# Attention of a decoder layer: 32 tiles one by one against 16 pairs of tiles, with query and scores in PSUM

## The chip, the cores and the metric

The kernel runs on one core of a Trainium2 chip. The metric is the time of one launch in device microseconds. A core has TensorE (matmul; PE in the profile, its weight loads PEld), VectorE (DVE), ScalarE (ACT), GpSimd (POOL) and SyncE (SP), which here issues DMAs.

## The reference

A decoder layer on x of 64 x 64 tokens with 256 features. Three blocks are added to x one after the other: windowed attention, cross-attention over a context, and a mixture of experts. The change touches the first block alone:

```python
Q = (_rmsnorm(x, g) @ _quant_w(wq).T).reshape(Bq, Lq, H, Dh)   # x is layer-normed first; H = Dh = 16
K = (x @ _quant_w(wk).T).reshape(Bq, Lq, H, Dh)
V = (x @ _quant_w(wv).T).reshape(Bq, Lq, H, Dh)
raw = jnp.arange(Lq)[:, None] - jnp.arange(W)[None, :] * STRIDE    # W = STRIDE = 8
valid = raw >= 0
attn = jnp.einsum('blhd,blwhd->bhlw', Q, Kg) * scale               # Kg = K[:, max(raw, 0)]
attn = attn + bias                                                 # -0.5 * log(8 w + 1)
attn = jax.nn.softmax(jnp.where(valid[None, None], attn, -jnp.inf), axis=-1)
out = jnp.einsum('bhlw,blwhd->blhd', attn, Vg).reshape(Bq, Lq, D)
return x + out @ _quant_w(wo).T
```

Every token sees itself and the tokens 8, 16, ... 56 positions before it: a dot product of 16 numbers for each of 16 heads and each lag, a softmax over at most 8 lags, and a weighted sum of values. `_quant_w` turns a weight matrix into -1, 0 and 1 times a scale.

## The kernel before

**Tiles.** 4096 tokens are 4 groups of 8 tiles of 128 tokens. In a group, tile p holds the tokens that stand p strides of 8 into their sequences, so that tile p attends to the tiles 0 to p of its own group. The width w = p + 1 runs from 1 to 8 in every group: 144 widths over the 32 tiles.

**Stages.** A tile goes through nine stages: STAT (mean and variance on VectorE), NORM, TRANS (transpose on TensorE, split into a high and a low part on ScalarE and GpSimd), QKV (ten matmuls into `ps_qk` and `ps_v`, copied out by ScalarE into `qk` and `v_sb`), PROD (`prod` = key times query for w tiles; GpSimd takes about 55% of the w tiles, VectorE the rest, both on line L237; then VectorE sums each run of 16 to `sraw`, L435), SOFT (score times its scale plus bias, L369; maximum over the lags, L379; subtraction, L392; exponential on ScalarE, L291; sum, reciprocal and normalisation, L412, L420, L428), PV (`pv` = value times weight for w tiles on GpSimd, L261), OT (2 w accumulating transposes on TensorE, L460, which add up the w tiles of `pv`), PROJ (output matrix, then VectorE adds the residual `u`, L424).

**Order.** Each engine runs a software pipeline written by hand: step a of group g works on tile n of the first stage, tile n - 1 of the second, and so on. An engine takes its instructions strictly in their written order, and waits at the first whose data isn't there. Counters (`Flow`, `f_...`) tell one engine that another is done. Group 0 and the last eight steps are written out, the groups between run in a loop. SyncE loads x tile by tile, issues the loads of the next phase (`prefetch`) in between, and stores x1 tile by tile.

**Scalars of a tile.** The normalisation needs a power of -0.5 (GpSimd, L275, a 128x2 instruction for each tile) and five 128x1 instructions on VectorE for each tile.

**After attention** an all-engine barrier stands, and then cross-attention and experts, which the change leaves as they are.

Of the kernel before, what the change touches and what calls it, by code (L numbers as in the profile page):

```python
# [21 lines left out]
P = 128  # L22
# [6 lines left out]
SHARE = 0.55  # L29
# [49 lines left out]
def attention_phase(nc, t, prefetch, prefetch_rows):  # L79

    ctx = ExitStack()
    with ctx:
# [3 lines left out]
        def pb(name, shape):  # L86
            return ctx.enter_context(nc.psum_tensor(name, shape, F32))

# [15 lines left out]
        XB = WIN  # L104
        w_raw = sb("w_raw", [P, 4, DC, D])
        w_neg = sb("w_neg", [P, DC, D])

        wq_f = sb("wq_f", [P, DC, D])
# [15 lines left out]
        mv = sb("mv", [P, WIN, 2])
        rs = sb("rs", [P, WIN, 4])
        rq = sb("rq", [P, WIN, 1])
        xh = sb("xh", [P, 2, D])
        u = sb("u", [P, WIN, D])
        qk = sb("qk", [P, 2, WIN, 2, D])
        v_sb = sb("v_sb", [P, 2, WIN, D])  # L130
        prod = sb("prod", [P, 2, WIN, D])
        sraw = sb("sraw", [P, 2, WIN, H])
        nm, rs1 = sb("nm", [P, WIN, 1]), sb("rs1", [P, WIN, 1])
        xt_hi, xt_lo = sb("xt_hi", [P, 2, DC, P], R32), sb("xt_lo", [P, 2, DC, P], R32)
        xt_f, ot = sb("xt_f", [P, 2, DC, P]), sb("ot", [P, 2, DC, P])
# [12 lines left out]

        s_const = sem("s_const")
        s_settled = sem("s_settled")  # L150
        s_wraw = sem("s_wraw")
        s_init = sem("s_init")
        s_wsum = sem("s_wsum")
        s_wtot = sem("s_wtot")
        s_wq = sem("s_wq")
        s_pool0 = sem("s_pool0")
        s_x = [sem(f"s_x{k}") for k in range(XB)]
        f_st = [flow(f"f_st{k}", 16) for k in range(WIN)]
        f_stat, f_rstd, f_xh = flow("f_stat", 4), flow("f_rstd"), flow("f_xh")
        f_rq = flow("f_rq", 2)  # L160
        f_u, f_tr, f_hi, f_lo = flow("f_u"), flow("f_tr"), flow("f_hi", 2), flow("f_lo")
        f_pqk, f_qk, f_v, f_nm = flow("f_pqk"), flow("f_qk"), flow("f_v"), flow("f_nm", 2)
        f_prod_g = flow("f_prod_g")
        f_prod, f_sm, f_exp = flow("f_prod", 2), flow("f_sm", 3), flow("f_exp")
        f_pn, f_pv, f_o = flow("f_pn", 3), flow("f_pv"), flow("f_o")
        f_ot, f_p, f_x1 = flow("f_ot"), flow("f_p"), flow("f_x1")

        def settle(eng):

            eng.sem_inc(s_settled, 1)  # L170

        N_CONST = 3
        w_ready = 12


        STAT, NORM, TRANS, QKV, PROD, SOFT, PV, OT, PROJ = range(9)
        DEPTH = PROJ

        def run(eng, step):

            for a in range(WIN):
                step(0, a, lambda k, a=a: a >= k)
            with eng.Fori(1, GRP) as g:
                for a in range(WIN):
                    step(g, a, lambda k: True)
            for a in range(DEPTH):
                step(GRP, a, lambda k, a=a: a < k)

        def at(g, a, k):

            return 8 * g + (a - k), (a - k) % WIN, g + (a - k) // WIN
# [3 lines left out]
        @block.sync  # L195
        def _(eng):
            open_flows(eng, flows)
            for i, name in enumerate(("wq", "wk", "wv", "wo")):
                eng.dma_start(w_raw[:, i, :, :], t[name].rearrange("(c p) o -> p c o", p=P)).then_inc(s_wraw, 16)
            eng.dma_start(g_col[:, :], t["g"]).then_inc(s_wraw, 16)  # L200
            eng.dma_start(ident[:, :], t["ident"]).then_inc(s_const, 16)
            eng.dma_start(bias_t[:, :, :], t["bias"]).then_inc(s_const, 16)
            eng.dma_start(ones[:, :], t["ones"]).then_inc(s_const, 16)

            def load(g, a):
                f_u.wait(eng, 8 * (g - 1) + a)
                eng.dma_start(x_in[:, a, :], t["x"][g, :, a, :]).then_inc(s_x[a], 16)

            def store(g, a):
                f_x1.wait(eng, 8 * g + a)  # L210
                eng.dma_start(t["x1"][g, :, a, :], u[:, a, :]).then_inc(f_st[a].sem, 16)

            for g in range(2):
                for a in range(WIN):
                    load(g, a)
                if g == 0:
                    prefetch(eng)
            with eng.Fori(2, GRP) as g:
                for a in range(WIN):
                    store(g - 2, a)  # L220
                    load(g, a)
            for a in range(WIN):
                f_st[a].wait(eng, GRP - 3)
            prefetch_rows(eng)
            with eng.Fori(GRP - 2, GRP) as g:
                for a in range(WIN):
                    store(g, a)
            for a in range(WIN):
                f_st[a].wait(eng, GRP - 1)

        def pool_share(v):

            return max(1, round(v * SHARE)) if v > 1 else 0

        def products(e, q, gg, lo, hi):

            return e.tensor_tensor(prod[:, q % 2, lo:hi, :], qk[:, gg % 2, lo:hi, 1, :],  # L237
                                   qk[:, gg % 2, q, 0, :].unsqueeze(1).to_broadcast([P, hi - lo, D]), ALU.mult)

        @block.gpsimd  # L240
        def _(eng):
            e = nc.gpsimd
            e.memset(power[:, :], -0.5).then_inc(s_pool0, 1)
            eng.wait_ge(s_pool0, 1)

            def step(g, a, valid):
                if valid(PROD):
                    m, q, gg = at(g, a, PROD)
                    if pool_share(q + 1):
                        f_qk.wait(eng, m)  # L250
                        f_prod.wait(eng, m - 2)
                        settle(eng)
                        f_prod_g.sig(products(e, q, gg, 0, pool_share(q + 1)))
                if valid(PV):
                    n, p, gg = at(g, a, PV)
                    w = p + 1
                    f_pn.wait(eng, n)
# [1341 lines left out]
```

## Time and profile before

| | us |
|---|---|
| median of 3 runs | 846.86 (846.11 to 847.08) |
| the profiled execution, its own time | 847.12 |
| its span, first to last instruction | 845.3 |
| last addition of the attention phase ends | 239.15 |
| first instruction of the next phase on ScalarE | 242.40 |

In the attention phase the profile's picture in 40 slices shows VectorE at nine tenths or more from the third slice to the tenth, TensorE at five to seven, GpSimd at five to eight. Busy time counts an instruction from its start to its end. A slice's digit is a mean over about 21 us.

### The profile page before, as it was taken

The page shows a single profiled execution, that of the slowest core. Times are in us where ns is not written, and L with a number is a line of the kernel's source. Part 1 is how long each engine was busy: PE and PEld are TensorE (multiplying, and loading weights), DVE is VectorE, ACT ScalarE, POOL GpSimd, SP SyncE. Part 2 cuts the span into 40 slices and gives each one's busy share as a digit, 9 for nine tenths or more (in the row PEclk, how much of TensorE's full clock was granted, in tenths as well). Part 3 has the DMA queues.
Part 4 walks back from the last instruction along what each step waited for, and adds up shares of the span by engine and source line. Part 5 has one row for each costly group of instructions (what it writes and reads, how often), then busy time and mean ns, then how long its engine had stood idle before and what let it go on. Part 6 is the DMA issues. An engine that isn't in the chain of part 4 may idle for free. (4 is left out here: it accounts for less than half of the span.)

```text
span 845.3 us, 19054 instructions
## 1 busy us (share of the span) xinstructions
PE 670.7 (79%) x4034; PEld 550.3 (65%) x4034; DVE 639.4 (76%) x2096; ACT 414.0 (49%) x1196; POOL 513.2 (61%) x403
## 2 busy tenths in 40 slices
PE   0766777667536789999986437899999999999994
PEld 0555666566424556665654316799999999998993
DVE  4699999999843577777665775777777777777773
ACT  0543545445113456554552145556666666666662
POOL 0587887877610006555777751577766775877775
PEclk9999989979877899999998778999999999999998
DMA  6811111300002334576334543577787786887774
GB/s 183 289 33 38 50 37 38 124 19 25 19 19 94 119 119 157 204 259 237 138 139 143 193 164 92 100 117 134 127 135 132 120 134 115 140 139 126 131 116 54
DMA packets 77614, 100.45 MB, mean 119 GB/s; under 512 B 10256, under 2 KB 70816, under 8 KB 76960
## 3 DMA queue, kind: packets, MB, share of 16 engines
q0 software_dynamic: 26736, 37.64, 24.8%
q1 hardware_dynamic: 50784, 61.74, 24.8%
q8 instruction: 37, 0.61, 0.3%
q14 instruction: 57, 0.47, 0.2%
HBM read 50.97 MB, written 52.95 MB: 123 GB/s over the span
## 5 line engine op out<-in xcount | busy, mean ns | idle before, releaser
L1480 POOL DMA_INDIRECT out_dram<-yw,xg x143 | 225.0, 1573 | 115.3 <-issue 55.1
L1079 POOL DMA_INDIRECT xs_scratch<-rows,slot x128 | 125.4, 980 | 131.2 <-issue 107.7
L1368 PE MATMUL cbank<-w,stc_hi 112*128 (+1 forms) x572 | 123.5, 309 | 2.9 <-issue 1.4
L1368 PE MATMUL cbank<-w_hi,xtc_hi 128*128 x286 | 105.6, 369 | 5.8 <-DVE xtc_lo L1380 5.6
L1368 PEld LDWEIGHTS cbank<-w,stc_hi 112*128 112x128 f32 (+1 forms) x572 | 88.8, 188 | 30.1 <-issue 23.6
L1380 DVE TENSOR_TENSOR xtc_lo<-cbank,xtc_hi 128x256 fp32r<-128x256 f32 x143 | 60.7, 424 | 46.1 <-ACT xtc_hi L1375 45.6
L1368 PE MATMUL cbank<-w_hi,xtc_lo 128*128 x286 | 92.7, 324 | 0.0
L460 PE MATMUL ps_o<-ident,pv 128*128 128x128 f32 x288 | 48.2, 326 | 55.9 <-ACT ot L296 50.4
L1368 PE MATMUL cbank<-w,xtc_hi 128*128 x286 | 92.5, 323 | 0.0
L1420 ACT ACTIVATE sgc<-hh 128x128 f32<-128x128 f32 x143 | 44.4, 310 | 92.3 <-DVE hh L1414 90.9
L460 PEld LDWEIGHTS ps_o<-ident,pv 128*128 128x128 f32 x288 | 40.0, 168 | 64.8 <-POOL pv L261 44.4
L1465 DVE TENSOR_SCALAR yw<-cbank,xg 128x256 f32<-128x256 f32 x143 | 68.8, 481 | 11.4 <-PE cbank L1368 6.9
L261 POOL TENSOR_TENSOR pv<-v_sb,pr 128x256 f32<-128x256 f32 (+7 forms) x32 | 69.4, 2169 | 6.4 <-DVE pr L428 6.4
L1357 PE MATMUL cbank<-identb,xg 128*128 128x128 f32 x286 | 55.4, 276 | 13.1 <-DMA xg<-xs_scratch 13.1
L1408 ACT ACTIVATE h<-cbank 128x176 f32<-128x176 f32 x143 | 45.4, 317 | 30.5 <-PE cbank L1368 28.5
L1368 PEld LDWEIGHTS cbank<-w_hi,xtc_hi 128*128 128x128 f32 x286 | 54.4, 190 | 8.8 <-issue 8.8
L291 ACT ACTIVATE pr<-sc 128x16 f32<-128x16 f32 (+7 forms) x32 | 8.4, 263 | 102.3 <-DVE sc L392 102.3
L1368 PEld LDWEIGHTS cbank<-w,xtc_hi 128*128 128x128 f32 x286 | 54.7, 191 | 0.0
L1368 PEld LDWEIGHTS cbank<-w_hi,xtc_lo 128*128 128x128 f32 x286 | 54.0, 189 | 0.0
L1414 DVE TENSOR_TENSOR hh<-cbank,h 128x176 f32<-128x176 f32 x143 | 48.9, 342 | 6.4 <-ACT h L1408 1.9
L1436 ACT ACTIVATE stc_hi<-cbank 128x256 fp32r<-128x256 f32 x143 | 53.5, 374 | 0.3 <-PE cbank L1430 0.3
L1375 ACT ACTIVATE xtc_hi<-cbank 128x256 fp32r<-128x256 f32 x143 | 52.2, 365 | 2.6 <-PE cbank L1357 2.4
(214 smaller groups left out, 1766.9 us busy)
## 6 DMA issues: line engine op xcount, KB each, us to landing
xg<-xs_scratch SPq DMA_DIRECT2D x143, 144.0 KB, 2.7
w<-w13r_dram SPq DMA_DIRECT2D x8, 704.0 KB, 6.1
x_in<-x_dram SPq DMA_DIRECT2D x32, 128.0 KB, 2.4
w_hi<-ctx_t_dram SPq DMA_DIRECT2D x8, 512.0 KB, 4.0
x_scratch<-u SPq DMA_DIRECT2D x32, 128.0 KB, 2.2
w_hi<-x_scratch SPq DMA_DIRECT2D x8, 512.0 KB, 4.0
out_dram<-w SPq DMA_DIRECT2D x16, 256.0 KB
w<-w2r_dram SPq DMA_DIRECT2D x4, 1024.0 KB, 9.9
```

The source lines that it names most:

```text
L261: f_pv.sig(e.tensor_tensor(pv[:, p % 2, 0:w, :].rearrange("p b (h d) -> p b h d", h=H), v_sb[:, gg % 2, 0:w, :].rearrange("p b (h d) -> p ...
L460: last = e.matmul(ps_o[:, ch * P:(ch + 1) * P], pv[:, p % 2, b, ch * P:(ch + 1) * P], ident[:, :], is_transpose=True, start=b == 0, stop=b ...
L1079: nc.gpsimd.indirect_dma_start(t["xs"], bass.IndirectOffsetOnAxis(ap=slot[:, n % 2, k:k + 1].bitcast(U32), axis=0), rows[:, n % NROW, k // ...
L1357: last = nc.tensor.transpose(R[p % 2][:, ch * P:(ch + 1) * P], xg[:, p, ch * P:(ch + 1) * P], ident[:, :])
L1368: last = nc.tensor.matmul(out, stationary, moving, start=j == 0, stop=j == len(pairs) - 1)
L1375: f["t_hi"].sig(nc.scalar.activation(xt_hi[:, p % 2, :, :], x_t(p), ACT.Copy))
L1380: f["t_ev"].sig(nc.vector.tensor_tensor(xt_lo[:, p % 2, :, :], x_t(p), xt_hi[:, p % 2, :, :].bitcast(F32), ALU.subtract))
L1408: f["h2"].sig(nc.scalar.activation(h2[:, p % 2, :], R[2 + p % 2][:, HID:2 * HID], ACT.Copy))
L1414: f["hh"].sig(nc.vector.tensor_tensor(hh[:, p % 2, :], R[2 + p % 2][:, 0:HID], h2[:, p % 2, :], ALU.mult))
L1436: f["st_hi"].sig(nc.scalar.activation(st_hi[:, p % 2, :, :], s_tr(p), ACT.Copy))
L1465: f["y_ev"].sig(nc.vector.tensor_scalar(yw[:, p % YB, :], R[6 + p % 2][:, 0:D], xg[:, p, bass.ds(c, 1)], None, ALU.mult))
L1480: nc.gpsimd.indirect_dma_start(t["out"], bass.IndirectOffsetOnAxis(ap=xg[:, p, ID:ID + 1].bitcast(U32), axis=0), yw[:, p % YB, :], None, c ...
```

## The change

The attention phase is written anew. Its parts:

1. Two tiles with the same p from two neighbouring groups form a pair; 16 pairs instead of 32 tiles. Each instruction of ScalarE and VectorE covers a pair where its form allows it (`[P, 2, ...]`), so half as many instructions carry twice the columns. Everything is written out, without a loop.
2. ScalarE writes the query, already times its scale, to PSUM (`ps_q`). The products of key (SBUF) and query (PSUM) are all made on VectorE (`scores`). The bias stands as a 17th number beside the 16 products of a head, so that the sum over 17 gives the finished score. Scores `sraw`, `den` and `rden` lie in PSUM (`ps_s`).
3. GpSimd keeps the values (`values`, one instruction for each tile), the low part of x transposed (`low`, a pair at once), and takes over all scalars of a tile: `root`, six small instructions for two pairs.
4. x, the residual and x1 share one ring of 12 pairs: ScalarE overwrites x in place (`residual`), VectorE adds in place (`add`), SyncE stores from it and loads the next pair 12 on.
5. Transposing x and adding up the values share the one bank `ps_t`. On ScalarE the two copies out of it for a pair (`turned`) stand first in a step.
6. The weights are loaded from ScalarE's queue, and their absolute sums are made by ScalarE (four instructions) instead of one instruction on VectorE.

```diff
-SHARE = 0.55
+PAIRS = TOK // (2 * P)
+QUAD, XR, KR, PVR = 2, 12, 11, 3
...
+        prod = sb("prod", [P, 2, WIN, H, DH + 1])
...
+        def evicted(eng, j):
+
+            at, _ = place(j)
+            f_root.wait(eng, j // QUAD)
+            f_pqk.wait(eng, j)
+            f_prod.wait(eng, j - 2, 1)
+            for a in range(2):
+                m = 2 * j + a
+                last = nc.scalar.activation(ps_q[:, j % 2, a * D:(a + 1) * D], ps_qk[:, a, 0:D], ACT.Identity, scale=rq[:, m:m + 1])
+            f_ev.sig(last)
...
+            f_ev.sig(nc.scalar.activation(k_sb[:, :, at, :], ps_qk[:, :, D:2 * D], ACT.Copy))
...
+            f_ev.sig(nc.scalar.activation(v_sb[:, :, at, :], two(ps_v), ACT.Copy))
...
+            f_prod.sig(e.tensor_tensor(
+                prod[:, :, 0:w, :, 0:DH], k_sb[:, :, at:at + w, :].rearrange("p t l (h d) -> p t l h d", h=H),
+                ps_q[:, j % 2, :].rearrange("p (t h d) -> p t h d", t=2, h=H).unsqueeze(2).to_broadcast([P, 2, w, H, DH]), ALU.mult))
+            f_prod.wait(eng, j, 1)
+            f_sm.wait(eng, j - 1)
+            f_prod.sig(e.tensor_reduce(sraw[:, :, 0:w, :], prod[:, :, 0:w, :, :], AX.X, ALU.add))
...
+        order = dict(
+            t=[(1, turn), (7, proj), (6, out_t), (2, qkv)],
+            s=[(1, turned), (6, out_te), (0, normed), (1, residual), (4, expo), (2, evicted)],
+            v=[(3, scores), (7, add), (0, look_ahead), (4, weigh)],
+            g=[(1, low), (0, root_at), (5, values)])
+
+        def run(eng, who):
+            for i in range(PAIRS + DEPTH):
+                for stage, what in order[who]:
+                    if 0 <= i - stage < PAIRS:
+                        what(eng, i - stage)
```

In `order`, (3, scores) means that step i of that engine works on pair i - 3. `look_ahead` (mean and variance) works on pair i + 3. `turn` is the transpose of x, `qkv` the twenty matmuls of a pair, `out_t` the 4 w transposes that add up the values, `out_te` their copy out of `ps_t`.

On VectorE, from the steps of width 2 and 3, before the change (the normalisation and product of one tile, then the sum and the scaling of the next):

```order
L392 TENSOR_TENSOR sc<-sc,mx 128x32
L396 TENSOR_SCALAR rq<-rq,qk_scale 128x1
L237 TENSOR_TENSOR prod<-qk 128x256
L408 BN_AGGR mv<-stats 128x2
L412 TENSOR_REDUCE den<-pr 128x16
L415 TENSOR_SCALAR rs<-mv 128x1
L416 TENSOR_SCALAR rs<-mv 128x1
L420 RECIPROCAL rden<-den 128x16
L428 TENSOR_TENSOR pr<-pr,rden 128x32
L435 TENSOR_REDUCE sraw<-prod 128x48
L369 SCALAR_TENSOR_TENSOR sc<-sraw,rq,bias_t 128x48
L376 BN_STATS stats<-x_in 128x6
```

The same place in the changed kernel, one whole step (`scores` of width 3, `look_ahead`, `weigh` of width 2; `ps_s` holds scores and sums):

```order
L293 TENSOR_TENSOR prod<-k_sb,ps_q 128x2x48x16
L298 TENSOR_REDUCE ps_s<-prod 128x2x48
L300 TENSOR_REDUCE mx<-ps_s 128x32
L303 TENSOR_TENSOR sc<-ps_s,mx 128x2x48
L166 BN_STATS stats<-x_ring 128x6 x2
L169 BN_AGGR mv<-stats 128x2 x2
L320 TENSOR_REDUCE ps_s<-pr 128x32
L322 RECIPROCAL ps_s<-ps_s 128x32
L324 TENSOR_TENSOR pr<-pr,ps_s 128x2x32
```

The product now covers all widths of two tiles, the scaling instruction (L369) and the 128x1 instructions are gone, and the four instructions of the scores stand back to back.

On GpSimd, two steps of group 0 before:

```order
L237 TENSOR_TENSOR prod<-qk 128x512
L261 TENSOR_TENSOR pv<-v_sb,pr 128x256
L269 TENSOR_TENSOR xt_lo<-xt_f,xt_hi 128x256
L275 TENSOR_TENSOR rs<-rs,power 128x2
L237 TENSOR_TENSOR prod<-qk 128x512
L261 TENSOR_TENSOR pv<-v_sb,pr 128x512
```

and in the changed kernel, the steps whose values have width 4 and 5:

```order
L335 TENSOR_TENSOR pv<-v_sb,pr 128x1024 x2
L246 TENSOR_TENSOR xt_lo<-xt_f,xt_hi 128x512
L189 TENSOR_TENSOR a_rs<-a_ve,power 128x2x4
L191 TENSOR_TENSOR nm<-a_ve,a_rs 128x4
L192 TENSOR_SCALAR rs<-a_rs 128x4
L193 TENSOR_TENSOR rq<-a_rs,a_ve 128x4
L195 TENSOR_TENSOR rq<-rq,a_rs 128x4
L198 TENSOR_SCALAR rq<-rq,qk_scale 128x4
L335 TENSOR_TENSOR pv<-v_sb,pr 128x1280 x2
```

The products are gone; in every second step six small instructions stand ahead of the two of the values.

On ScalarE, one whole step of the changed kernel (`turned`, `out_te`, `normed`, `residual`, `expo`, `evicted`):

```order
L238 ACTIVATE xt_hi<-ps_t 128x512
L240 ACTIVATE xt_f<-ps_t 128x512
L359 ACTIVATE ot<-ps_t 128x512
L211 ACTIVATE xh<-x_ring,nm,a_rs 128x256 x2
L222 ACTIVATE x_ring<-x_ring,nm,rs 128x256 x2
L311 ACTIVATE pr<-sc 128x2x64
L276 ACTIVATE ps_q<-ps_qk,rq 128x256 x2
L280 ACTIVATE k_sb<-ps_qk 128x2x256
L283 ACTIVATE v_sb<-ps_v 128x2x256
```

The copies of the next pair's transpose follow right behind the four evictions of a pair.

## Rows read from the trace of the kernel before

**Rows 1.** Busy time of each engine by stretch; PEclk is the granted clock.

```profile
core 0: us, PE busy (x) PEld busy (x) DVE busy (x) ACT busy (x) POOL busy (x), PEclk, DMA share, GB/s
20.00:240.00 220.00, 153.58 (x800) 129.26 (x800) 202.00 (x545) 91.55 (x256) 160.86 (x124) 0.90 0.21 67
40.00:220.00 180.00, 128.05 (x697) 108.45 (x695) 177.68 (x457) 79.22 (x223) 143.52 (x111) 0.90 0.14 44
```

**Rows 2.** Who waited for whom, 40 to 220 us: total, times, longest.

```profile
ACT pr L291 <- DVE sc L392: 90.1, 26, 5.1
```

**Rows 3.** Timeline around 132 us: start, duration, engine, line.

```profile
132.09 3.69 POOL L261 TENSOR_TENSOR pv<-v_sb,pr 128x2048 f32<-128x2048 f32 x1
132.17 3.63 DVE L392 TENSOR_TENSOR sc<-sc,mx 128x16 f32<-128x16 f32 x1
```

**Rows 4.** VectorE's groups by line and shape, attention phase: busy us, mean ns.

```profile
L376 DVE BATCH_NORM_STATS2 stats<-x_in 128x6 f32<-128x256 f32 x32 | 13.4, 417 | 0.0
L392 DVE TENSOR_TENSOR sc<-sc,mx 128x16 f32<-128x16 f32 x4 | 10.8, 2710 | 0.0
L392 DVE TENSOR_TENSOR sc<-sc,mx 128x128 f32<-128x128 f32 x4 | 1.1, 280 | 0.0
L237 DVE TENSOR_TENSOR prod<-qk 128x1024 f32<-128x1024 f32 x1 | 1.2, 1218 | 0.0
L237 DVE TENSOR_TENSOR prod<-qk 128x256 f32<-128x256 f32 x3 | 1.3, 425 | 2.5 <-ACT qk L314 2.5
L435 DVE TENSOR_REDUCE sraw<-prod 128x128 f32<-128x2048 f32 x4 | 9.1, 2279 | 0.0
L435 DVE TENSOR_REDUCE sraw<-prod 128x16 f32<-128x256 f32 x4 | 1.6, 407 | 0.0
L379 DVE TENSOR_REDUCE mx<-sc 128x16 f32<-128x128 f32 x4 | 1.4, 352 | 0.0
L420 DVE RECIPROCAL rden<-den 128x16 f32<-128x16 f32 x32 | 7.9, 247 | 0.2
```

**Rows 5.** Line L424, one operand in PSUM: duration in ns, shortest, median, longest.

```profile
L424 DVE SCALAR_TENSOR_TENSOR u<-ps_p,vo_scale,u x32: 385/392/484, 50.6 to 238.7; 128x256 f32<-128x256 f32 x32
```

**Rows 6.** GpSimd's groups by line and shape, attention phase.

```profile
L269 POOL TENSOR_TENSOR xt_lo<-xt_f,xt_hi 128x256 fp32r<-128x256 f32 x32 | 24.7, 772 | 35.9 <-ACT xt_f L304 35.9
L275 POOL TENSOR_TENSOR rs<-rs,power 128x2 f32<-128x2 f32 x32 | 22.4, 699 | 21.9 <-DVE rs L416 21.9
L261 POOL TENSOR_TENSOR pv<-v_sb,pr 128x2048 f32<-128x2048 f32 x4 | 14.7, 3682 | 2.6 <-DVE pr L428 2.6
L261 POOL TENSOR_TENSOR pv<-v_sb,pr 128x256 f32<-128x256 f32 x4 | 2.5, 616 | 0.0
```

**Rows 7.** TensorE's timeline: one tile's ten QKV matmuls early and late, transposes, projection.

```profile
25.72 0.76 PE L484 MATMUL ps_qk<-wqk,xt_hi 128*128 128x512 f32 x1
...
28.63 0.41 PE L488 MATMUL ps_v<-wv_t,xt_lo 128*128 128x256 f32 x1
...
133.56 0.67 PE L484 MATMUL ps_qk<-wqk,xt_hi 128*128 128x512 f32 x1
...
135.35 0.28 PE L488 MATMUL ps_v<-wv_t,xt_lo 128*128 128x256 f32 x1
...
234.02 1.97 PE L460 MATMUL ps_o<-ident,pv 128*128 128x128 f32 x16 [0.47 <-POOL pv L261]
...
235.83 1.03 PE L450 MATMUL ps_p<-wo_t,ot 128*128 128x256 f32 x4
```

**Rows 8.** ScalarE's groups, 0 to 305 us.

```profile
L309 ACT ACTIVATE xh<-x_in,nm,rs 128x256 f32<-128x256 f32 x32 | 19.5, 610 | 7.0 <-DVE nm L385 7.0
L314 ACT ACTIVATE qk<-ps_qk 128x512 f32 x24 | 14.4, 602 | 3.8 <-PE ps_v L488 3.7
```

**Rows 9.** Timeline: last weight ready; last addition of attention; then loads of x.

```profile
19.66 0.75 DVE L357 SCALAR_TENSOR_TENSOR wo_t<-w_raw,whalf,w_neg 128x512 f32<-128x512 f32 x1
...
238.67 0.48 DVE L424 SCALAR_TENSOR_TENSOR u<-ps_p,vo_scale,u 128x256 f32<-128x256 f32 x1 [1.29 <-PE ps_p L450]
```

**Rows 10.** Loads of x, from issue to landing.

```profile
DMA to landing us min/median/max: 2.4/2.4/3.4
```

More of the change, by code:

```diff
@@ L150, in attention_phase @@
[L150 to L161, printed above, removed]
@@ new lines, in turn, with turned @@
+        def turn(eng, j):
+            f_xh.wait(eng, j)
+            f_ot.wait(eng, j - 6)
+            for a in range(2):
+                for ch in range(DC):
+                    last = nc.tensor.transpose(two_t(ps_t)[:, a, ch, :], xh[:, a, ch * P:(ch + 1) * P], ident[:, :])
+            f_tr.sig(last)
+        def turned(eng, j):
+            f_tr.wait(eng, j)
+            f_pqk.wait(eng, j - 2)
+            f_hi.sig(nc.scalar.activation(xt_hi[:, j % 2, :, :, :], two_t(ps_t), ACT.Copy))
+            f_lo.wait(eng, j - 1)
+            f_hi.sig(nc.scalar.activation(xt_f[:, :, :, :], two_t(ps_t), ACT.Copy))
@@ new lines, in out_t @@
+        def out_t(eng, j):
+            _, w = place(j)
+            if j + 5 < PAIRS:
+                f_hi.wait(eng, j + 5)
+            f_ot.wait(eng, j - 1)
+            for a in range(2):
+                m = 2 * j + a
+                f_pv.wait(eng, j, a + 1)
+                for ch in range(DC):
+                    for l in range(w):
+                        last = nc.tensor.matmul(two_t(ps_t)[:, a, ch, :], pv[:, m % PVR, l, ch * P:(ch + 1) * P], ident[:, :],
+                                                is_transpose=True, start=l == 0, stop=l == w - 1)
+                f_o.sig(last)
@@ new lines, in out_te, with proj @@
+        def out_te(eng, j):
+            f_o.wait(eng, j)
+            f_p.wait(eng, j - 1)
+            f_ot.sig(nc.scalar.activation(ot[:, :, :, :], two_t(ps_t), ACT.Copy))
+        def proj(eng, j):
+            if j == 0:
+                eng.wait_ge(s_wq, O_READY)
+            f_ot.wait(eng, j)
+            f_x1.wait(eng, j - 1)
+            for a in range(2):
+                for ch in range(DC):
+                    last = nc.tensor.matmul(ps_p[:, a * D:(a + 1) * D], ot[:, a, ch, :], wo_t[:, ch, :], start=ch == 0, stop=ch == DC - 1)
+            f_p.sig(last)
@@ L203, in _ @@
[L203 to L233, printed above, removed]
@@ L235, in products @@
-        def products(e, q, gg, lo, hi):
-            return e.tensor_tensor(prod[:, q % 2, lo:hi, :], qk[:, gg % 2, lo:hi, 1, :],
-                                   qk[:, gg % 2, q, 0, :].unsqueeze(1).to_broadcast([P, hi - lo, D]), ALU.mult)
+            for j in range(QUAD, 2 * QUAD):
+                load(eng, j)
+            prefetch(eng)
+            for j in range(2 * QUAD, XR):
+                load(eng, j)
+            for j in range(PAIRS - XR):
+                store(eng, j)
+                load(eng, j + XR)
@@ L277, in _ @@
-            run(eng, step)
+            root(eng, 0)
+            run(eng, "g")
         @block.scalar
@@ L438, in _ @@
[L438 removed]
+            assert c == K_READY
+            ternary(2, wv_t[:, :, :])
+            assert c == V_READY
+            ternary(3, wo_t[:, :, :])
+            assert c == O_READY
+            run(eng, "v")
         @block.tensor
         def _(eng):
[L442 to L446 removed]
@@ L491, in _ @@
-            run(eng, step)
+            eng.wait_ge(s_wraw, 16 * 7)
+            eng.wait_ge(s_const, 16)
+            eng.wait_ge(s_wsum, 4)
+            nc.tensor.matmul(ps_p[:, 0:4], ones[:, :], wsum[:, :], start=True, stop=True).then_inc(s_wtot, 1)
+            run(eng, "t")
 class TileTable:
```

475 lines of the change are left out of this document (208 added, 267 removed).

## The prediction, as it was put on record

> **What bounds the kernel now.** I read the busy time by stretch first. From 40 to 220 us VectorE is busy for 177.68 of 180 us, TensorE for 128.05, GpSimd for 143.52, ScalarE for 79.22 [rows 1]. So VectorE sets the pace of attention. The waits agree: ScalarE's exponential waits 90.1 us for VectorE's subtraction L392 [rows 2]. Then VectorE's groups by shape: L392 on 16 columns takes 2710 ns, on 128 columns 280 ns [rows 4]. A narrow instruction can't cost ten times a wide one by its own work. The timeline has the reason: L392 on 16 columns starts at 132.17 and ends at 135.80, while GpSimd's `pv` runs from 132.09 to 135.78 [rows 3]. VectorE, with two operands in SBUF, stands until GpSimd's instruction is over, and that counts as busy. L424, with one operand in PSUM, never takes more than 484 ns over all 32 tiles, although GpSimd is busy four fifths of the time [rows 5, 1]. So VectorE's busy time holds its own work and such stalls, and the change puts one operand of nearly every such instruction into PSUM.
>
> **VectorE after the change.** From the two ends of each shape I take a price as fixed part plus columns [rows 4]: products 0.16 us + 1.03 ns a column, sums 0.14 us + 1.045 ns. A small instruction costs about 0.15 us. The maximum, whose operand is read with a step, costs 352 ns for 128 columns, so about 1.6 ns a column. For a pair of width w: products cover 512 w columns (0.53 w us), the sum over 17 covers 544 w (0.57 w), maximum 0.05 w, subtraction 0.03 w, four fixed parts 0.6. **Scores: 0.6 + 1.18 w**, 10.0 us at w = 8. **Weigh**: sum, reciprocal (247 ns for 16 columns, I take 0.35 for 32) and product: 0.65 + 0.086 w. **Add**: 392 ns for 256 columns [rows 5], so 0.65 for 512. **Look**: two statistics of 417 ns, two small ones and half of three small ones: 1.4. Over 16 pairs, whose widths sum to 72, this is 16 x (0.6 + 0.65 + 0.65 + 1.4) + 72 x 1.27 = 144 us, against 202 busy between 20 and 240 [rows 1]. All products are on VectorE now and it still needs 58 us less: the stalls and the 128x1 instructions go. Unknown are products written in runs of 16 with a pitch of 17, and PSUM read with a step; the trace has no such row. From below I take 1.03 ns (all runs of 16 in one piece), from above the 1.6 ns of the stepped maximum. I take the lower, because a run of 16 is still in one piece and the sum's is a whole one.
>
> One rule speaks for the upper end. The row shows 1.6 ns a column for a read where each column is 64 bytes from the last [rows 4]. The Trainium skill, page "SBUF — State Buffer", section "Door 1: The DMA port swizzle", says that SBUF is laid out in lines of 16 bytes and that each access that crosses to a new line pays a penalty; runs with a pitch of 17 numbers start off such a line. By the rule the products would stand nearer to the upper price, and the sum would be that of the pitch rival below; by the row of unbroken runs it stays at 144 us.
>
> **TensorE after the change.** The same matmuls. One tile's QKV takes 25.72 to 29.04 early, 3.3 us, and 133.56 to 135.63 later, 2.1 us [rows 7]; a pair 6.6 or 4.2. Sixteen transposes take 1.97 us, so `out_t` 0.49 w a pair; projection 2.06; `turn` 0.5 to 0.6. A pair costs 6.9 + 0.49 w, in all 145 us: as much as VectorE. It was hidden before; now it decides where w is small. ScalarE joins it into a chain: after a pair's QKV come the query's two copies, key, value (0.5, 0.5, 0.6, 0.6) and `turned`, twice 0.6 [rows 8]. Only then may `out_t` go on, since it shares the bank `ps_t`. TensorE has `turn` and the projection (2.7 us) to fill these 3.4. **Chain of a step: 4.2 + 3.4 + 0.2 of handovers = 7.8, plus 0.49 w** of the pair then in `out_t`. GpSimd at w = 8: two values of 3.68, `low` about 1.36 for 512 columns, and half of `root`. `root` has one power on 8 columns, between 0.7 and 2.8 us (0.699 for 2 columns), and five small ones [rows 6]. That is 10 to 12 us, under VectorE's 13.3.
>
> **The clock time of it.** Weights are ready at 20.4 [rows 9]. I move this by under 1 us: four ScalarE instructions of about 0.6 take the place of one. GpSimd's `low` for pair 0 follows two `normed` and two `turned` and ends near 22; `turn` of pair 1 ends near 22.8. QKV of pair 0 at the slow rate ends at 29.4, query and key are out at 31.0. The first three steps are bound by QKV and eviction at the slow rate (6.6 + 2.1 + 0.2 = 8.9), the next by the same at the fast one (6.6): scores of pairs 0 to 3 start at 31.0, 39.9, 48.8, 55.4. Then VectorE's step (scores, add, look, weigh) or the chain, whichever is longer: 8.2, 9.4, 10.7, 12.0 put pairs 4 to 7 at 63.6, 73.0, 83.7, 95.7. At the wrap from w = 8 to w = 1 the projection waits for the add behind the wide scores (10.7), then projection, `out_t` of width 6, QKV and two copies (10.7): pair 9 starts at 117.1. Chains with `out_t` of widths 7, 8, 1, 2: 11.0, 11.5, 8.2, 8.6 (pairs 10 to 13 at 128.1, 139.6, 147.8, 156.4). Then VectorE, without `look`, again: 9.3, 10.6, 11.8, so its last wide step ends at 188.1. **The tail** is serial: add, projection, `out_t` of pair 13 and its copy, exponential and weigh of pair 15 (to about 194), GpSimd's four values of widths 7 and 8 (to 202), 16 transposes, copy, projection, add: 207.6. For handovers that a table of this kind leaves out I add 3 us, my choice: 210.6. It is 239.15 now [rows 9]. **Saved: 28.5 us.** Stores are 256 KB instead of 128 KB, for which the 3 us have room. The profiled execution took 847.12, so 818.6; it lies 0.26 over the median of the runs. I predict **818.4**. What follows attention is untouched.
>
> The x loads of pairs 4 to 11 stand behind the prefetch in SyncE's queue. I cost that at nothing: loads of 128 KB land 2.4 to 3.4 us after issue, also in the first 40 us [rows 10], and the first steps have 8.9 us each. Without that cover a late load would hold VectorE ahead of all scores, up to some 8 us.
>
> **Rivals.** *Lockstep, as above*: 0.66, own range 810 to 830. *More overlap*: the engines run ahead further than a step, and VectorE alone counts. Its steps of pairs 0 to 15 add up to 129.5 us, which would end the last wide step at 160.5 instead of 188.1; half way is 14 us less, **804**. For it: three engines have queues of pairs between them. Against: `ps_p`, `ps_t` and `ps_qk` are single. Chance 0.12.
>
> *New stalls on VectorE*: `look` ends with three 128x4 `tensor_scalar` with both ends in SBUF, in six batches during the loop. If each batch meets a values instruction as L392 does (3.6 us at most, rows 3), it costs 22 us at worst, **840**. The same time comes out if GpSimd's small instructions cost much more than I think. The 128x1 ones never met this, but one column may be a special case. The Trainium skill, page "SBUF — State Buffer", section "Who interferes with whom", says that `tensor_scalar` can enter a mode that takes both port pairs and then contends with GpSimd; the trace shows such stalls with two-operand instructions alone. Chance 0.13.
>
> *The other side, pitch*: products and sums at 1.6 ns a column instead of 1.04, 0.6 us more per width and pair, 43 us in all. VectorE then bounds every step: 31.0 + 129.5 + 43 + 19.5, and the first three steps, where QKV still binds, add about 11, and the wrap about 11 more: last add near 245, **853**, slower by 0.7%. It decides from about 0.45 ns a column on. For it the stepped maximum, against it each unbroken run of 16. Chance 0.07; 0.02 remain for other things.
>
> **Range.** 800 to 838 takes in lockstep, more overlap and half of the stalls; pitch and the worst of the stalls stay out. Faster by over 0.2% (about what a measurement here can tell from no change): 0.91; within: 0.02; slower: 0.07.
>
> **What the profile would show.** Right: no VectorE instruction of the loop takes much more than its columns ask for; products of width 8 near 4.3 us, sums near 4.5; TensorE waits for ScalarE at the transposes where w is small and VectorE waits for ScalarE's key there, with VectorE without gaps at widths 6 to 8; a granted clock at or above today's 0.90; last add near 210. Wrong: products of width 8 over 6 us (pitch), `tensor_scalar` of 128x4 in microseconds (stalls), GpSimd without gaps, or VectorE waiting for a load of x ahead of the first scores.

## The result and the profile after

The changed kernel takes 808.17 us, median of 4 runs (805.45 to 809.12); the kernel before took 846.87 beside it. The ratio is 0.954, with a 95% interval of 0.952 to 0.956. The profiled execution took 807.66 us, its span is 805.9. The prediction was 818.4 us with a range of 800 to 838; it missed the time by 10 us, more than a third of what it said would be saved (28.5 us). The time also lies outside the 810 to 830 that the prediction gave its main case, *lockstep*.

The last addition of attention ends at 201.82 + 0.75 = 202.57 us, and ended at 239.15 before [rows 9]: 36.6 us of the 39.5 between the two profiled executions. The other 3 us lie behind attention, in code that was not changed, and I have not followed them up.

Windows of the changed kernel, to set beside [rows 1]; columns as there:

```profile
core 0: us, PE busy (x) PEld busy (x) DVE busy (x) ACT busy (x) POOL busy (x), PEclk, DMA share, GB/s
20.00:40.00 20.00, 14.75 (x72) 12.43 (x72) 6.08 (x25) 12.70 (x27) 7.72 (x10) 1.00 1.03 327
40.00:180.00 140.00, 104.54 (x608) 91.34 (x608) 128.10 (x171) 72.52 (x158) 86.27 (x77) 0.91 0.13 42
180.00:205.00 25.00, 18.80 (x116) 16.25 (x116) 6.36 (x12) 2.10 (x4) 13.81 (x4) 0.91 0.16 53
```

VectorE is busy for 128.10 of 140 us in the middle, but for 6.08 of 20 us ahead of it. The waits of the changed kernel, 20 to 205 us (engine, line, releaser; total, times, longest), say why, and what the middle still waits for:

```profile
ACT ot L359 <- PE ps_t L351: 69.8, 16, 13.1
...
PE ps_p L369 <- DVE x_ring L376: 26.0, 9, 7.7
POOL pv L335 <- DVE pr L324: 17.8, 5, 6.3
DVE stats L166 <- DMA x_ring<-x_dram: 13.6, 1, 13.6
...
DVE x_ring L376 <- PE ps_p L369: 13.3, 4, 5.4
```

The fourth row is one wait of 13.6 us, for a load of x. The last is the serial tail: all four of these waits stand behind 182 us. Then VectorE's groups by shape, 40 to 180 us, to set beside [rows 4, 5] (busy us, mean ns):

```profile
L298 DVE TENSOR_REDUCE ps_s<-prod 128x256 f32<-128x4352 f32 x2 | 9.4, 4695 | 0.1
L293 DVE TENSOR_TENSOR prod<-k_sb,ps_q 128x4096 f32<-128x4096 f32 x2 | 8.8, 4414 | 0.0
...
L376 DVE SCALAR_TENSOR_TENSOR x_ring<-ps_p,vo_scale,x_ring 128x512 f32<-128x512 f32 x11 | 8.2, 741 | 0.0
...
L293 DVE TENSOR_TENSOR prod<-k_sb,ps_q 128x1024 f32<-128x1024 f32 x2 | 2.4, 1205 | 0.3 <-ACT k_sb L280 0.3
...
L303 DVE TENSOR_TENSOR sc<-ps_s,mx 128x256 f32<-128x256 f32 x2 | 0.8, 424 | 0.1
```

Products: (4414 - 1205) / 3072 = 1.04 ns a column, with the pitch of 17 and the query in PSUM. L303, which has taken the place of the subtraction that took 2710 ns on 16 columns [rows 4], takes 424 ns on 256. One group still has the old form. The timelines of VectorE and of GpSimd at 120 us (start, duration):

```profile
118.37 7.35 POOL L335 TENSOR_TENSOR pv<-v_sb,pr 128x2048 f32<-128x2048 f32 x2
...
120.34 1.76 DVE L174 TENSOR_SCALAR a_ve<-mv 128x4 f32<-128x4 f32 x1
122.01 0.16 DVE L175 TENSOR_SCALAR a_ve<-mv 128x4 f32<-128x4 f32 x1
122.08 3.66 DVE L176 TENSOR_SCALAR a_ve<-mv 128x4 f32<-128x4 f32 x1
```

The two instructions of the values run from 118.37 to 125.72, about 3.7 us each. L174 ends with the first (122.10), L176 with the second (125.74). A `tensor_scalar` on 4 columns, both ends in SBUF, stands like the subtraction in [rows 3]; the same operation on one column, L388 and L396 of the kernel before, never took more than 0.27 us. By the Trainium skill, page "SBUF — State Buffer", section "Who interferes with whom", VectorE and GpSimd share one pair of ports as an exclusive lock, and `tensor_scalar` can be among the users; these rows agree.

### The profile page after: what moved, and what is told of

Same layout as the page of the kernel before. It is cut to its first block and busy times, and to the rows that moved or that the text cites. A ratio compares the mean times of both kernels' runs of the same rounds, so it can differ in the third digit from the quotient of the medians.

```text
span 805.9 us, 17540 instructions
## 1 busy us (share of the span) xinstructions
PE 654.5 (81%) x4034; PEld 541.0 (67%) x4034; DVE 575.0 (71%) x1769; ACT 413.8 (51%) x1140; POOL 461.8 (57%) x375
## 3 DMA queue, kind: packets, MB, share of 16 engines
q0 software_dynamic: 26736, 37.64, 25.8%
## 5 line engine op out<-in xcount | busy, mean ns | idle before, releaser
L335 POOL TENSOR_TENSOR pv<-v_sb,pr 128x256 f32<-128x256 f32 (+7 forms) x32 | 68.4, 2158 | 18.4 <-DVE pr L324 17.8
L1367 PE MATMUL cbank<-identb,xg 128*128 128x128 f32 x286 | 55.4, 276 | 13.1 <-DMA xg<-xs_scratch 13.1
L369 PE MATMUL ps_p<-wo_t,ot 128*128 128x256 f32 x128 | 36.6, 436 | 28.1 <-DVE x_ring L376 26.0
L1418 ACT ACTIVATE h<-cbank 128x176 f32<-128x176 f32 x143 | 45.5, 318 | 22.6 <-PE cbank L1378 18.7
L369 PEld LDWEIGHTS ps_p<-wo_t,ot 128*128 128x128 f32 x128 | 26.4, 217 | 34.5 <-issue 28.0
L246 POOL TENSOR_TENSOR xt_lo<-xt_f,xt_hi 128x512 fp32r<-128x512 f32 x16 | 20.9, 1308 | 44.5 <-ACT xt_f L240 44.5
```

What stands on the lines that cost most here:

```text
L335: f_pv.sig(nc.gpsimd.tensor_tensor(pv[:, m % PVR, 0:w, :].rearrange("p l (h d) -> p l h d", h=H), v_sb[:, a, at:at + w, :].rearrange("p l ...
L369: last = nc.tensor.matmul(ps_p[:, a * D:(a + 1) * D], ot[:, a, ch, :], wo_t[:, ch, :], start=ch == 0, stop=ch == DC - 1)
L1367: last = nc.tensor.transpose(R[p % 2][:, ch * P:(ch + 1) * P], xg[:, p, ch * P:(ch + 1) * P], ident[:, :])
L1418: f["h2"].sig(nc.scalar.activation(h2[:, p % 2, :], R[2 + p % 2][:, HID:2 * HID], ACT.Copy))
```

## The experiments

There were twelve runs in three groups of four. The first two groups ran on chips on which the kernel before took 905.6 and 905.4 us; the third on one where it took 845.5. So ratios go by each group's own runs of the kernel before, and the same saving in microseconds is a smaller share on the first two. The 60 us between the chips lie behind attention: the changed kernel's last addition ends within 3 us on the chip of its first profile and on that of the second group. For attention I compare the end of its last addition in the profiled execution. Two executions of the unchanged kernel gave 202.57 and 199.61, so one such number is good to some 3 us. The clock made this difference: from 104 to 108 us it was granted at 0.50 in the first execution and at 1.00 in the second. A projection of 8 matmuls took 3.75 us there against 1.97, the 24 transposes behind it 3.84 against 2.78. The scores of pair 8 start at 105.87 and 106.29, those of pair 9 at 115.64 and 112.65. Each experiment on placement moves data between PSUM and SBUF and leaves the arithmetic as it is.

**The ledger of all kernels**

| kernel | last addition ends | median us | ratio, 95% interval |
|---|---|---|---|
| before | 239.15 | 846.87 | 1 |
| before, products all on VectorE | 228.66 | 833.92 | 0.986 (0.984 to 0.988) |
| before, softmax data in PSUM | 211.79 | 884.64 | 0.972 (0.960 to 0.983) |
| before, both | 207.45 | 813.37 | 0.962 (0.960 to 0.964) |
| changed | 202.57 | 808.17 | 0.954 (0.952 to 0.956) |
| changed, again | 199.61 | 867.16 | 0.957 (0.952 to 0.961) |
| changed, query in SBUF | 204.27 | 870.54 | 0.959 (0.950 to 0.969) |
| changed, softmax data in SBUF | 203.67 | 874.58 | 0.966 (0.957 to 0.975) |
| changed, both in SBUF | 207.77 | 878.37 | 0.965 (0.953 to 0.977) |
| changed, bulk stores late | 194.20 | 860.92 | 0.949 (0.944 to 0.954) |
| changed, addition first | 198.04 | 862.41 | 0.955 (0.950 to 0.959) |
| changed, small ones on GpSimd | 201.22 | 866.80 | 0.952 (0.946 to 0.957) |
| stores late, addition first | 192.99 | 796.98 | 0.942 (0.940 to 0.944) |
| the same, small ones on GpSimd | 191.31 | 798.95 | 0.946 (0.943 to 0.949) |

Two ratios don't go by all executions. *Addition first* leaves out the profiled one, 844.98 us, which is 14 us under the other five; with it the ratio is 0.950. *Small ones on GpSimd* leaves out 873.71 (the profiled one) and 870.31; with them it is 0.955.

### 1. Undoing the placement in the changed kernel, and doing it alone in the kernel before

```diff
-        ps_q = ctx.enter_context(nc.psum_tensor("ps_q", [P, 2, 512], F32))
+        ps_q = w_raw[:, 0:2, :, :].rearrange("p w c o -> p w (c o)")
...
-        ps_t, ps_v, ps_p, ps_s = (ctx.enter_context(nc.psum_tensor(n, [P, 512], F32)) for n in ("ps_t", "ps_v", "ps_p", "ps_s"))
+        ps_t, ps_v, ps_p = (ctx.enter_context(nc.psum_tensor(n, [P, 512], F32)) for n in ("ps_t", "ps_v", "ps_p"))
+        ps_s = w_raw[:, 2, :, :].rearrange("p c o -> p (c o)")
```

Query in SBUF. 

> The changed kernel with the scaled query in SBUF (in the place of the raw weights) instead of PSUM; all else as it is. Theory 'stalls' (a VectorE instruction with two SBUF operands stands until GpSimd's running instruction is over, and the other way round): each of the 16 products meets a values instruction in about six cases of ten and waits 1 to 3 us, and GpSimd waits for long products too; 10 to 25 us slower than the changed kernel, 818 to 833. Rival 'fewer instructions' (the gain is from pairing, PSUM does nothing): 806 to 811.

Scores, sums and reciprocals in SBUF. 

> The changed kernel with scores, sums and reciprocals in SBUF instead of PSUM, the query still in PSUM. 'Stalls': the subtraction and the normalisation of a pair (32 instructions) each wait 0.5 to 1.5 us in the mean; part of it lies in steps that TensorE bounds; 6 to 20 us slower, 814 to 828. 'Fewer instructions': 806 to 811.

Both. 

> Both of the above: query, scores, sums and reciprocals in SBUF. 'Stalls': 18 to 40 us slower than the changed kernel, 826 to 848, so that most of the gain over the kernel before is gone. 'Fewer instructions': 806 to 811.

And in the kernel before, the placement alone:

```diff
+        ps_s, ps_c = pb("ps_s", [P, 512]), pb("ps_c", [P, 512])
+        sraw = ps_s[:, 0:2 * WIN * H].rearrange("p (t b h) -> p t b h", t=2, b=WIN)
+        rden = ps_s[:, 2 * WIN * H:2 * WIN * H + H]
+        sc = ps_c[:, 0:WIN * H].rearrange("p (b h) -> p b h", b=WIN)
```

> The kernel before with one part of the change alone: sraw, sc and rden in PSUM, so that L369, L392 and L428 have one SBUF operand. Nothing else moves. 'Stalls': these three lines are busy for about 75 us and need 24 by the prices of the rows; VectorE loses some 50 us, of which GpSimd and TensorE let 20 to 40 through: 807 to 827. 'Fewer instructions': within 5 us of the kernel before, 842 to 850.

In the kernel before, the placement alone brings 27.4 of the 36.6 us (211.79 against 239.15), inside the 20 to 40 that the theory of the stalls gave. VectorE's groups of that kernel, 20 to 240 us:

```profile
L238 DVE TENSOR_TENSOR prod<-qk 128x256 f32 (+7 forms) x32 | 52.7, 1645 | 2.4 <-issue 1.2 <-ACT qk L315 0.7
...
L370 DVE SCALAR_TENSOR_TENSOR ps_c<-ps_s,rq,bias_t 128x16 f32<-128x16 f32 (+7 forms) x32 | 9.6, 301 | 1.1
...
L393 DVE TENSOR_TENSOR ps_c<-ps_c,mx 128x16 f32<-128x16 f32 (+7 forms) x32 | 7.5, 234 | 0.1
```

The subtraction falls from 36.1 us (in the same view of the kernel before) to 7.5 and the scaling from 25.8 to 9.6. But the products, which still have two operands in SBUF, grow from 28.0 to 52.7: the stall moves on to the next instruction of its kind. At 74.37 a product on 256 columns takes 3.79 us and ends with GpSimd's values:

```profile
74.19 3.68 POOL L262 TENSOR_TENSOR pv<-v_sb,pr 128x2048 f32<-128x2048 f32 x1
...
74.37 3.79 DVE L238 TENSOR_TENSOR prod<-qk 128x256 f32 x1
```

In the changed kernel the undoing costs far less than I had expected: 4.7, 4.1 and 8.2 us against the 199.61 of the later profile, 1.7, 1.1 and 5.2 against 202.57. Only the last of the three is more than two profiles of one kernel can differ, and by the ratios none is told from the changed kernel, since the intervals overlap. The busy times and the timelines show more. So the theory is right on what stalls are, and wrong on who pays. The reason stands in the timelines around the widest product. First the changed kernel, then the one with the query in SBUF:

```profile
92.68 4.42 DVE L293 TENSOR_TENSOR prod<-k_sb,ps_q 128x4096 f32<-128x4096 f32 x1
92.84 5.59 POOL L335 TENSOR_TENSOR pv<-v_sb,pr 128x1536 f32<-128x1536 f32 x2 [1.21 <-DVE pr L324]
```

```profile
94.17 4.42 DVE L293 TENSOR_TENSOR prod<-k_sb,w_raw 128x4096 f32<-128x4096 f32 x1
94.34 9.69 POOL L335 TENSOR_TENSOR pv<-v_sb,pr 128x1536 f32<-128x1536 f32 x2 [0.85 <-DVE pr L324]
```

VectorE's product takes 4.42 us in both. GpSimd's pair of instructions takes 5.59 us in the one and 9.69 in the other, 4.1 more: here GpSimd stands until VectorE's product is over. Whoever comes second pays. VectorE's `weigh` releases the values, and its next instruction is the product, so VectorE is mostly first. GpSimd's groups of this kernel, 20 to 205 us, show the same in sum; values were 68.4, the low parts 20.9 and the powers 11.7 in the changed kernel:

```profile
L335 POOL TENSOR_TENSOR pv<-v_sb,pr 128x256 f32<-128x256 f32 (+7 forms) x32 | 83.2, 2620 | 7.8 <-DVE pr L324 7.2 <-PE ps_t L351 0.6
L246 POOL TENSOR_TENSOR xt_lo<-xt_f,xt_hi 128x512 fp32r<-128x512 f32 x16 | 28.4, 1776 | 26.3 <-ACT xt_f L240 26.3
L189 POOL TENSOR_TENSOR a_rs<-a_ve,power 128x8 f32<-128x8 f32 x7 | 16.0, 2291 | 10.4 <-DVE a_ve L176 10.4
```

GpSimd is busy 26.6 us more in these three groups and VectorE 2.8 us more in its products (40.8 to 43.6). GpSimd waited 44.5 us for ScalarE's copies, and now for 26.3, so 18.2 of the 26.6 us are taken from that idle time. With the scores in SBUF the stalls are few: the subtraction, 4.9 us in all, becomes 9.0. At width 8 it starts 9 us and more after the release of the values, when GpSimd has ended.

### 2. Where the products stand

The kernel before with all products on VectorE, alone and with the placement of experiment 1:

```diff
         def pool_share(v):
-            return max(1, round(v * SHARE)) if v > 1 else 0
+            return 0
```

> The kernel before with all products on VectorE; GpSimd keeps the low halves, the powers and the weighed values. Nothing is placed in PSUM. Theory B (each engine's stall is the price of two long instructions with two SBUF operands that meet; GpSimd sheds about 37 us of products and can no longer meet VectorE with them, VectorE takes some 37 us more work): the last addition, 239.2 in the kernel before, ends at 225 to 240, VectorE's 128x16 subtraction of the maximum falls from 2.7 us to under 2. Rival (the split matters by itself, the stalls were from the products): under 220. Rival (VectorE's added work is simply added): over 245.

With the placement as well: 

> The kernel before with all products on VectorE and with raw scores, scores and reciprocals in PSUM: the change without pairs of tiles, without the scaled query in PSUM and without the ring. Last addition 211.8 for the placement alone, 199.6 for the changed kernel on this chip. Theory B (placement and split do the work against stalls, pairs save the fixed cost of instructions, some 190 x 0.2 us on VectorE): 205 to 215. Rival (pairs add nothing more): 198 to 202. Rival (VectorE is the bound without pairs and pays for the products): over 218.

The last addition ends at 228.66 and 207.45, both inside the range of the first theory. To take 47.6 us of products off GpSimd and give them to VectorE, the engine that bounds, makes the kernel faster by 1.4%. VectorE's groups without the placement, 20 to 240 us:

```profile
L237 DVE TENSOR_TENSOR prod<-qk 128x1280 f32 (+15 forms) x32 | 43.4, 1355 | 2.8 <-ACT qk L314 1.7 <-issue 0.8
...
L369 DVE SCALAR_TENSOR_TENSOR sc<-sraw,rq,bias_t 128x16 f32<-128x16 f32 (+7 forms) x32 | 27.7, 866 | 1.1
L392 DVE TENSOR_TENSOR sc<-sc,mx 128x16 f32<-128x16 f32 (+7 forms) x32 | 15.2, 474 | 0.1
```

VectorE takes 15.4 us more of products (28.0 to 43.4) and sheds 20.9 in the subtraction (36.1 to 15.2). By the prices of [rows 4] its old share, 68 of the 144 widths, needs 23.1 us, so 4.9 of the old 28.0 were stall; the other 76 need 20.0, which makes 43.1. I had put the narrow form of the subtraction at under 2 us; it took 2188 ns. On 112 columns the subtraction took 1514 ns before and 263 here. So GpSimd's products, too, had stood in VectorE's way. With the placement too, the kernel stands 4.9 to 7.8 us behind the changed one. That is what pairs, query in PSUM and the ring bring together, as they stand, and no run takes these three apart. Part of what they bring is given back at the start (experiment 3).

### 3. The loads behind the prefetch

The prefetch for later phases holds, beside weights, three bulk stores from DRAM to DRAM. They go out ahead of the loads of x for pairs 4 to 11. The experiment takes them out of the prefetch and issues them behind these loads:

```diff
             prefetch(eng)
             for j in range(2 * QUAD, XR):
                 load(eng, j)
+            prefetch_pads(eng)
```

> The changed kernel once more, unchanged, as the baseline of this group of runs. Both theories: its last addition ends near 202.6 us (+-1), as in its first profile, and its ratio to the kernel before is 0.95 to 0.96.

> The three bulk stores of the prefetch (pads of the expert phase) are issued after the loads of x for pairs 4 to 11 instead of ahead of them. Theory A (the 13.6 us in which VectorE waited for pair 4's x is the queue behind these stores, and delays the pipeline only until TensorE's own pace is reached): the wait falls under 3 us, scores of pair 1 start near 40, but those of pair 4 (61.4 us in the changed kernel) come at most 2 us earlier, and the last addition moves from 202.6 to 200.5 to 202. Rival (the wait is on the path throughout): the last addition moves by 8 us or more, to 190 to 195. Rival (the stores are then late for what follows the attention): the last addition moves, the whole time doesn't or gets longer by up to 3 us.

The unchanged kernel came out at 199.61, outside the 202.6 +-1 that I had expected, and at 0.957. My own theory on the stores, a gain of 2 us at most, missed; the rival with 190 to 195 holds the 194.20. The end is 5.4 us earlier than in the repeated profile and 8.4 earlier than in the first, and the ratio falls from 0.957 to 0.949, with intervals that overlap at their ends. VectorE's timeline in the changed kernel, and in this one:

```profile
22.94 0.16 DVE L176 TENSOR_SCALAR a_ve<-mv 128x4 f32<-128x4 f32 x1
36.71 0.75 DVE L166 BATCH_NORM_STATS2 stats<-x_ring 128x6 f32<-128x256 f32 x2 [13.60 <-DMA x_ring<-x_dram]
...
39.06 0.68 DVE L293 TENSOR_TENSOR prod<-k_sb,ps_q 128x512 f32<-128x512 f32 x1
```

```profile
25.44 0.16 DVE L176 TENSOR_SCALAR a_ve<-mv 128x4 f32<-128x4 f32 x1
28.92 0.69 DVE L293 TENSOR_TENSOR prod<-k_sb,ps_q 128x512 f32<-128x512 f32 x1 [3.33 <-ACT k_sb L280]
...
34.41 1.22 DVE L293 TENSOR_TENSOR prod<-k_sb,ps_q 128x1024 f32<-128x1024 f32 x1 [2.65 <-ACT k_sb L280]
```

The scores of pair 0 start at 28.92 instead of 39.06. The cause is in the queue's own rows. SyncE's timeline in the changed kernel, then here:

```profile
18.54 16.89 SPq L385 DMA_DIRECT2D x_ring<-x_dram  x8
```

```profile
16.62 5.77 SPq L385 DMA_DIRECT2D x_ring<-x_dram  x8
```

Eight loads take SyncE 16.89 us to issue behind the stores and 5.77 ahead of them. The first of the eight, pair 4's, takes 9.76 us of the 16.89, to 28.30, and VectorE's statistic of it starts 8.4 us later, at 36.71. The eight take 8.5 to 9.1 us from issue to landing, against 2.4 to 3.4 in [rows 10]. So this load is late twice over, in its issue and in its landing. Ten microseconds of lead shrink to 5 or 8 at the end: pairs 0 to 3 take 16.9 us here (28.92 to 45.82), and 13.9 in the changed kernel, where pairs 1 and 2 have been through TensorE already when VectorE comes to them.

### 4. The order of the addition, and the small instructions

```diff
-            v=[(3, scores), (7, add), (0, look_ahead), (4, weigh)],
+            v=[(7, add), (3, scores), (0, look_ahead), (4, weigh)],
```

> In VectorE's order of a step the addition of pair i-7 stands ahead of the scores of pair i-3 instead of behind them. Theory A (TensorE's 26.0 us of waits for the ring of the sum are slack in the wide steps, where VectorE is never idle): these waits fall below 10 us, the last addition moves by -1 to +1 us. Rival (they are on the path): the last addition ends 3 to 8 us earlier. Rival (VectorE now waits for the projection at the narrow steps): VectorE's 13.3 us of waits for the projection grow to over 20 us, and the last addition ends 2 to 6 us later.

The end moves by -1.6 us against the repeated profile, no more than two profiles of one kernel differ, and the ratio of five of the six executions doesn't move (0.955). It is none of my three outcomes. The two waits trade: TensorE's for the ring falls from 27.5 us to 13.4, and VectorE's for the projection rises from 13.3 to 18.7.

Then the three 128x4 instructions, taken out of `look` on VectorE and put on GpSimd, in `root`, ahead of the powers (the first of them; the other two alike):

```diff
-                f_ve.sig(e.tensor_scalar(ve[:, 0, s], mv[:, s, 1], LN_EPS, None, ALU.add))
+            f_ve.sig(e.tensor_scalar(ve[:, 0, s], mv[:, s, 1], LN_EPS, None, ALU.add))
```

> The three 128x4 additions and products that prepare the roots run on GpSimd in place of VectorE. VectorE's own cost of them is 8.5 us between 20 and 205 us, of which 3 x 0.16 x 7 = 3.4 us would be left without a stall. Theory A (the stalls behind GpSimd's long instruction, 1.76 and 3.66 us at 120 us, lie on VectorE's path): VectorE is busy 8 us less and the last addition ends 3 to 6 us earlier. Rival (they lie ahead of waits for the scalar engine that take them up): it moves by less than 1 us. Rival (GpSimd's three more instructions, about 0.5 us each ahead of the powers, delay the roots and so the scalar engine): it ends 1 to 4 us later.

VectorE is busy 123.73 us from 40 to 180 instead of 128.10 in the first profile and 132.21 in the repeated one, but the end stands at 201.22, between the two unchanged ones. So no gain is to be seen; that VectorE would have waited in that time anyhow is my reading, and no run shows it.

The combinations, which are also the versions to keep:

> The changed kernel with the bulk stores behind the loads and the addition ahead of the scores. Last addition 199.6 unchanged, 194.2 with the first edit, 198.0 with the second (one profile each; two profiles of the unchanged kernel differ by 3 us). If the two gains add, 191 to 193.5 and a ratio to the kernel before of 0.946 to 0.950; if the second is only the spread of GpSimd's meeting points, 194 to 197 and 0.949 to 0.953.

> The same with the three 128x4 instructions ahead of the powers on GpSimd too. VectorE sheds 6 to 8 us of work, of which 3.4 us are not stalls. If that lies on VectorE's path once the loads are early: last addition 1 to 4 us earlier than without it; if GpSimd's longer chain to the roots takes it back: the same within 1 us, or up to 2 us later.

Stores late and addition first ends at 192.99 and takes 796.98 us, 0.942 of the kernel before and 1.2% under the changed kernel's 0.954, with intervals apart. The 192.99 lies in the case in which both gains add (191 to 193.5), and the ratio is below both cases. But the end is only 1.2 us ahead of the stores alone, less than two profiles of one kernel differ, so whether the order of the addition brings anything beyond the stores stays open. The small instructions moved to GpSimd make the end 1.7 us earlier in one profile and the median 2 us later: no gain to be seen. Of the three edits, only the stores have a gain that is clear of the spread.

## Why the prediction was right, and where not

**What bounds the kernel, and the stalls: right.** VectorE's stalls behind GpSimd were the time to be had. Split alone brings 10.5 us, placement alone 27.4, both 31.7, all of the change 36.6 or 39.5.

**VectorE's sum: right.** I gave 144 us. The groups of lines L166 to L376 between 20 and 205 us add up to 145.2 us; by the window, to set beside the 202 of [rows 1], it is 140.5. The terms: products 4.4 us at width 8 and sums 4.7, as the prices give them (4.3 and 4.5 in the signs), addition 0.74 against 0.65, reciprocal 0.37 against 0.35. The maximum with its step, read from PSUM, took 0.42 for 256 columns, where 1.6 ns a column and 0.15 give 0.56.

**Pitch, the rival on the other side: refuted.** 1.04 ns a column, the price of an unbroken run; the upper price of 1.6 ns is not seen. The rule on lines of 16 bytes that I took from the Trainium skill, page "SBUF — State Buffer", section "Door 1: The DMA port swizzle", spoke for that upper price, and the products written with a pitch of 17 show no such cost.

**"I cost that at nothing" (the x loads of pairs 4 to 11): wrong, by the 8 us named beside it.** Scores of pair 0 start at 39.06, not 31.0, and VectorE waited for a load of x ahead of them, which I had named as a sign of being wrong. I had costed a load by its landing in [rows 10], and left out both the time that SyncE needs to issue it behind the bulk stores and the slower landing there. The first of the two stood in the trace of the kernel before, whose loads follow the same three stores. SyncE's time for each load, first before and then changed (ns, shortest, median, longest):

```profile
L207 SPq DMA_DIRECT2D x_in<-x_dram x32: 327/338/6741, 6.5 to 160.0; - x32
```

```profile
L385 SPq DMA_DIRECT2D x_ring<-x_dram x16: 368/702/9758, 2.6 to 105.8; - x16
```

The longest of the first line, 6.74 us from 25.77 on, is the first load behind the stores.

**"Chain of a step: 7.8 + 0.49 w": too long, by 14 us in sum.** Starts of the scores by pair, as predicted and as found in the changed kernel:

| pair | 0 | 3 | 7 | 9 | 12 | 15 |
|---|---|---|---|---|---|---|
| predicted | 31.0 | 55.4 | 95.7 | 117.1 | 147.8 | 176.3 |
| measured | 39.06 | 52.96 | 92.68 | 115.64 | 141.88 | 170.06 |

Pairs 0 to 3 took 13.9 us instead of 24.4, pairs 9 to 12 took 26.2 instead of 30.7. Where VectorE bounds, from 3 to 7, it is 39.7 against 40.3. The early steps show which term was off. TensorE's timeline in the kernel with the stores late, where no load is in the way: the first QKV matmul of pair 1, its last, the transposes behind it, and the first of pair 2.

```profile
29.45 0.47 PE L261 MATMUL ps_qk<-wqk,xt_hi 128*128 128x512 f32 x1 [1.66 <-ACT v_sb L283]
...
32.67 0.29 PE L265 MATMUL ps_v<-wv_t,xt_lo 128*128 128x256 f32 x1
...
35.02 0.47 PE L261 MATMUL ps_qk<-wqk,xt_hi 128*128 128x512 f32 x1 [1.62 <-ACT v_sb L283]
```

Twenty matmuls take 3.5 us, where I had 6.6 at the slow rate and 4.2 at the fast one, doubled from single tiles [rows 7]. The step is 35.02 - 29.45 = 5.6 us instead of 8.9. I had taken the slow rate for the first three pairs because the kernel before runs at it in its first tiles. But the change of rate comes at another time in the changed kernel. Its own TensorE timeline, in the matmuls of pair 0:

```profile
24.54 0.63 PE L264 MATMUL ps_qk<-wqk,xt_lo 128*128 128x512 f32 x1
...
27.44 0.39 PE L264 MATMUL ps_qk<-wqk,xt_lo 128*128 128x512 f32 x1
```

TensorE had worked without a gap since 21.08, and went from the lower of its two levels (1.2 GHz) to the upper one (2.4 GHz) at about 27. In the kernel before, whose tiles have gaps of 0.6 us and more between them there, the same matmul still takes 0.63 us at 36.96, and 0.39 at 39.41. (The granted clock reads 1.00 from 20 to 40 us in both, so that column doesn't show it.) In the changed kernel even the short step was hidden: pairs 1 and 2 went through TensorE while VectorE waited for the load.

From 9 to 12 the chain has the form that I gave it, but each step is some 1.5 us too long. TensorE starts the matmuls of a pair at 120.15, 130.07, 136.92 and 144.21, steps of 9.9, 6.9 and 7.3 us, where 7.8 + 0.49 w gives 11.7, 8.3 and 8.8. In the widest of them the twenty matmuls take 3.4 us (4.2), the stretch of ScalarE's copies 3.1 (3.4 and 0.2) and the 32 transposes 3.5 (3.9). So the constant is nearer to 6.4 than to 7.8: it was mis-sized. That the engines run further ahead than a step, the rival *more overlap*, is not what these rows show, though its 804 is nearer to the measured 808.2 than my 818.4.

**Tail and handovers.** From the last wide `weigh` (182.05) to the end it takes 20.5 us, predicted 19.5. The 3 us that I added for handovers were not needed. The account from 210.6 to 202.6: +8.1 late start, -14.3 shorter steps from pair 0 to 15, +0.2 and +1.0 behind them, -3.0 handovers. Two errors of 8 and 14 us stood against each other; that attention came out only 8 us from the forecast is in part luck. The remaining 2.9 us (818.6 against 807.66 for a profiled execution) lie behind attention, and their cause is open.

**New stalls of `look`: seen, but small.** The three 128x4 instructions take 8.5 us in all (10.8 in the repeated profile) where 3.4 would do without stalls: 5.1 or 7.4, not 22. Single ones did take microseconds, 1.76 and 3.66, another of my signs of being wrong; but in most batches they met no values instruction, and experiment 4 finds no gain in their removal.

## What to carry to other kernels

When VectorE and GpSimd both work from SBUF, look up in the timeline who comes second. That one pays, and the busy time of a narrow instruction shows it. Put one operand of VectorE's instructions in PSUM, or let the stall fall on the engine with idle time. If one instruction is cured alone, look where the stall went next.

Cost a load by its place in the queue: what is issued ahead of it, how large, and how long the engine needs to issue it. Look for the longest issue and not for the median. Its time to landing in a quiet stretch is not enough.

## What the runs showed of the hardware that I had not expected

The stall goes both ways: a VectorE product of 4.42 us with both operands in SBUF kept GpSimd's values waiting for 4.1 us, and with one operand in PSUM it did not.

An engine's issue of DMAs can stand: eight loads of 256 KB took SyncE 16.89 us behind three bulk stores (4.4 MB), 9.76 of them for the first, and 5.77 us ahead of them.

TensorE's rate can change while the granted clock reads 1.00: 0.63 us for a matmul on 512 columns at 24.54 and 0.39 at 27.44, with the engine at work without a gap.

VectorE's stepped read from PSUM is priced like a whole run: the maximum over 256 columns took 0.42 us, and 0.58 us in the run with the same scores in SBUF.
